# A state space layer reordered: norm, bias and rotation in PSUM banks, fewer steps per angle, another loop order

## The reference, cut to what matters

```
Bm, Cm = rmsnorm(x @ WB.T) * Bn_w + B_bias, rmsnorm(x @ WC.T) * Cn_w + C_bias     # per head, 128 columns
dt, lam = softplus(x @ Wdt.T), sigmoid(x @ Wlam.T)
angle = cumsum over t of (x @ Wth.T) * dt
Bm, Cm = rope(Bm, angle), rope(Cm, angle)
alpha = exp(-dt * exp(A_log)); beta = (1 - lam) * dt * alpha; gamma = lam * dt
h[t] = alpha[t] h[t-1] + beta[t] B[t-1] x[t-1]' + gamma[t] B[t] x[t]'
y[t] = C[t] . h[t]
out = (y * silu(z)) @ Wout.T,   z = x @ Wz.T;   x = x + out
```

## Time and profile before

| | us |
|---|---|
| median of 3 runs (1844.03 to 1847.19) | 1845.42 |
| the profiled execution, its own time | 1846.38 |
| its span | 1844.7 |
| TensorE busy | 1529.5 (83%) |
| VectorE busy | 1137.8 (62%) |
| ScalarE busy | 863.2 (47%) |
| GpSimd busy | 498.3 (27%) |

### The profile page before, as it was taken

How to read it: one execution, slowest core, us unless ns; L and a number is a source line. 1 busy time by engine, 2 the same in 40 slices (tenths; PEclk the granted TensorE clock), 3 DMA queues, 4 the chain that set the end, 5 groups by cost and what they waited for, 6 DMA issues and landing times. The chain is left out here.

```text
span 1844.7 us, 25358 instructions
## 1 busy us (share of the span) xinstructions
PE 1529.5 (83%) x8808; PEld 1090.0 (59%) x8808; DVE 1137.8 (62%) x2334; ACT 863.2 (47%) x1937; POOL 498.3 (27%) x515
## 2 busy tenths in 40 slices
PE   7869888589968995746999999999976688888768
PEld 5643444367645784644877787777832255555567
DVE  5778998356745545553456644444439678888833
ACT  2548898311335421222434442333324578888711
POOL 2350000000000031014243233224000288888810
PEclk9978999789979997577999999999989889999969
DMA  3007999554032001030000000000022222223010
GB/s 126 1 1 138 180 187 177 154 169 155 27 67 59 24 1 35 15 118 1 1 1 1 1 1 1 1 1 1 1 91 89 89 70 83 90 78 94 1 48 27
DMA packets 190491, 110.89 MB, mean 60 GB/s; under 512 B 150121, under 2 KB 166505, under 8 KB 189468
## 3 DMA queue, kind: packets, MB, share of 16 engines
q1 hardware_dynamic: 190364, 109.26, 23.0%
HBM read 75.41 MB, written 0.26 MB: 41 GB/s over the span
## 5 line engine op out<-in xcount | busy, mean ns | idle before, releaser
L670 DVE TENSOR_REDUCE x_row_max<-banks 128x1 f32<-128x512 f32 x248 | 152.6, 682 | 16.3 <-PE banks L364 16.2
L210 PE MATMUL banks<-a_w_ring,x_normed_T 128*128 128x512 f32 x320 | 151.2, 613 | 13.2 <-DVEq L2916 5.6
L2870 POOL TENSOR_TENSOR a_t<-a_t,a_bias_ring 128x512 f32<-128x512 f32 x64 | 126.4, 1996 | 129.5 <-DVE a_t L2942 129.3
L573 ACT ACTIVATE x_v_full<-banks,x_neg_max,x_q_scale 128x1024 int16<-128x1024 f32 x128 | 153.4, 1202 | 16.6 <-DMA x_v_full<-x_v_full 7.5
L2215 PE MATMUL banks<-x_v,x_expsT 128*128 128x128 f32 x1088 | 148.6, 277 | 10.8 <-ACT x_expsT L2373 5.9
L2215 PEld LDWEIGHTS banks<-x_v,x_expsT 128*128 128x128 f32 x1088 | 134.0, 192 | 15.3 <-ACT x_expsT L2373 7.3
L2493 DVE TENSOR_REDUCE x_small<-banks 128x1 f32<-128x2048 f32 x32 | 73.3, 2292 | 86.2 <-PE banks L2196 86.2
L2300 POOL TENSOR_TENSOR x_t<-x_t 128x512 f32<-128x512 f32 (+1 forms) x48 | 54.4, 1134 | 259.9 <-DVE x_t L2475 259.9
L2196 PE MATMUL banks<-x_kT,x_qT 128*128 128x512 f32 x256 | 118.6, 607 | 4.7 <-ACT x_exps L2355 4.7
L364 PE MATMUL banks<-x_kT_parts,x_qT_int 64*128 64x512 bf16 x512 | 103.9, 409 | 5.4 <-DVE x_row_max L670 2.6
L210 PEld LDWEIGHTS banks<-a_w_ring,x_normed_T 128*128 128x128 f32 x320 | 59.9, 195 | 79.9 <-issue 67.8
(11 more groups left out here) (531 smaller groups left out, 3595.2 us busy)
## 6 DMA issues: line engine op xcount, KB each, us to landing
a_w_ring<-in_L_attn_WB_T SPq DMA_DIRECT2D x16, 512.0 KB
a_w_ring<-in_L_attn_WC_T SPq DMA_DIRECT2D x16, 512.0 KB
f_w_gate_up<-in_L_ffn_gate_up SPq DMA_DIRECT2D x18, 352.0 KB
ctx_tokens<-in_ctx SPq DMA_DIRECT2D x16, 256.0 KB, 5.6
a_w_ring<-in_L_attn_Wth_T SPq DMA_DIRECT2D x8, 512.0 KB
a_bias_ring<-in_L_attn_B_bias_perm SPq DMA_DIRECT2D x16, 256.0 KB
a_bias_ring<-in_L_attn_C_bias_perm SPq DMA_DIRECT2D x16, 256.0 KB
f_w_down<-in_L_ffn_down SPq DMA_DIRECT2D x18, 176.0 KB
```

What stands on the lines that cost most here:

```text
L210: last = nc.tensor.matmul(out, lhsT, rhs, start=(i == 0), stop=(i == len(pairs) - 1))
L573: nc.scalar.activation(eb[:, q % RING], k.ps[:, 2 + 2 * (q % 2):4 + 2 * (q % 2), :].rearrange("p a n -> p (a n)"), ACT.Exp, bias=nb[:, v % ...
L670: nc.vector.reduce_max(mx[:, u % 2, i:i + 1], k.bank(MBANK[m % 3]), AX.X).then_inc(s.max_taken, 1)
L2870: last = nc.gpsimd.tensor_tensor(a, a, bring[:, i % RB, j], ALU.add).then_inc(s.bias_used, 1)
```

## The change

`l3_attn` is rewritten.

- The layer norm is inside the same block; the semaphores of the stage before are cleared by SP between loads (the two pools are swapped). DMA order: dt weights, A_log, Wz, ring pieces 0 and 1, Wx, piece 2, norm weights, Wout, clears, the rest.
- z is projected before theta 0 and 1, x after; weighting x and gating z are done between blocks of angles.
- Angles are in turns (dt divided by two pi once), so that the reduction is one rounding and one difference.
- Norm and bias are computed in place in the banks, both by VectorE, and the rotation reads the banks; `t1` goes. The sine product is one 512-column operation instead of two of 256 for each of B and C; GpSimd takes the halves crosswise.
- The root is a power of -0.5 on GpSimd, with the variance made by a copy on ScalarE; reciprocal and square root go. GpSimd masks E with a select.
- The diagonal of G isn't multiplied by TensorE: ScalarE sums each row of the diagonal matrix (accumulated copy), VectorE multiplies x_diag by it and adds it as it takes y.
- The order of the loop changes on every engine; three quarters of the output's gate, transposes and projection come before the last units end.

Its core (removed lines mostly left out):

```diff
-    BC_BANKS = ((1, 2), (0, 5))
+    HN = N4 // 2
+    CH = DIN // P
+    LAST = NG4 // CH * (CH - 1) * B
+    BC_BANKS = ((5, 6), (0, 1))
+    TH_BANKS, CUM_BANKS = (0, 1), (2, 3)
+    X_BANKS, Z_BANKS = (5, 4), (7, 6)
+    TURN_BANK, DECAY_BANK, G_BANK, Y_BANK = 3, 4, 2, 7
+    old = k.swap_pools()
...
+                for sem in old:
+                    sp.sem_clear(sem)
+                for i in range(3, NTH + NG4):
+                    piece(i)
...
+                def total_angle(q):
+                    pe.wait_ge(s.thdt_ready, q + 1)
+                    if q >= 2:
+                        pe.wait_ge(s.cum_taken, q - 1)
+                    nc.tensor.matmul(k.bank(CUM_BANKS[q % 2]), k.keep[:], thdt[:, q % 2], start=True, stop=True).then_inc(s.cum_in_psum, 1)
...
+                for q in range(NTH * B):
+                    total_angle(q)
+                    if q == 1:
+                        pe.wait_ge(s.ww_ready, 1)
+                        x_of(1)
+                    if q + 2 < NTH * B:
+                        theta(q + 2)
...
+                    for j in range(2):
+                        if n >= 2:
+                            pe.wait_ge(s.roped, 2 * (n - 2) + j + 1)
+                        matmul_acc(nc, k.bank(BC_BANKS[n % 2][j]), [(k.xt[:, c, tokens[b]], ring[:, i % RB, j, c]) for c in range(DC)]).then_inc(s.bc_in_psum, 1)
+                    if b == B - 1:
+                        pe.wait_ge(s.bc_in_psum, 2 * (n + 1))
+                        pe.sem_inc(s.w_used, 1)
...
+                def read_out(m):
+                    g, b = divmod(m, B)
+                    pe.wait_ge(t.e_masked, m + 1)
+                    if m >= 1:
+                        pe.wait_ge(t.y_taken, m)
+                    for h in range(HG):
+                        hh = g * HG + h
+                        last = nc.tensor.matmul(k.bank(Y_BANK, P, P4, h * P4), ee[:, m % 4, h * P:(h + 1) * P], xw[:, b, hh * P4:(hh + 1) * P4], start=True, stop=True)
+                    last.then_inc(t.y_in_psum, 1)
...
+                project(0)
+                for n in range(NU):
+                    if n == 0:
+                        pe.wait_ge(s.cum_taken, NTH * B)
+                    if n + 1 < NU:
+                        project(n + 1)
...
+                    if n >= 1:
+                        turn_over(n - 1, 0)
+                    decay(n)
+                    if n >= 1:
+                        turn_over(n - 1, 1)
                     if n >= 2:
+                        read_out(n - 2)
+                    if n >= 1:
+                        products(n - 1)
+                pe.wait_ge(t.yz_ready, B)
+                pe.wait_ge(s.roped, 2 * NU)
+                turn_over(NU - 1, 0)
+                y_turn(0, (0, 1))
+                turn_over(NU - 1, 1)
+                y_turn(1, (2,))
+                read_out(NU - 2)
+                products(NU - 1)
+                pe.wait_ge(k.w_loaded[10], 3 * 16)
+                pe.wait_ge(t.yT_ready, 2)
+                y_project((0, 1))
+                read_out(NU - 1)
+                y_project((2,))
+                pe.wait_ge(t.yz_ready, 2 * B)
+                y_turn(TURN_BANK, (3,))
+                pe.wait_ge(t.yT_ready, 3)
+                y_project((3,)).then_inc(t.y_out, 1)
...
+                    nc.scalar.activation(cosine, cosine, ACT.Sin, bias=quarter[:, 0:1], scale=-2.0 * PI_IN).then_inc(s.trig_done, 1)
+                    nc.scalar.activation(sine, sine, ACT.Sin, scale=2.0 * PI_IN).then_inc(s.trig_done, 1)
...
+                    act.wait_ge(s.sq_done, n + 1)
+                    nc.scalar.activation(st[:, r, 1], st[:, r, 0], ACT.Copy, bias=RMS_EPS, scale=1.0 / N4).then_inc(s.var_ready, 1)
...
+                def diagonal(m):
+                    act.wait_ge(t.e_masked, m + 1)
+                    if m >= 1:
+                        act.wait_ge(t.gd_ready, m)
+                    if m >= 2:
+                        act.wait_ge(t.gx_ready, m - 1)
+                    for h in range(HG):
+                        last = nc.scalar.activation(junk[:, 2, h * P:(h + 1) * P], dg[:, m % 2, h * P:(h + 1) * P], ACT.Copy, accum_out=gt[:, m % 2, h:h + 1])
+                    last.then_inc(t.gd_ready, 1)
+                act.wait_ge(s.ww_ready, 1)
+                decays(0)
+                squares(0)
+                for n in range(NU):
+                    if n >= 3:
+                        diagonal(n - 3)
                     if n + 1 < NU:
+                        decays(n + 1)
                         squares(n + 1)
+                    if n >= 1:
+                        take_turned(n - 1, 0)
+                    exponentials(n)
+                    if n >= 1:
+                        take_turned(n - 1, 1)
+                diagonal(NU - 3)
...
+                def root(n):
+                    pool.wait_ge(s.var_ready, n + 1)
+                    nc.gpsimd.tensor_tensor(st[:, n % 2, 2], st[:, n % 2, 1], neg_half[:], ALU.pow).then_inc(s.rstd_ready, 1)
+
+                def add_rotated(m):
+                    for j in range(2):
+                        pool.wait_ge(s.roped, 2 * m + j + 1)
+                        for hf, op in ((0, ALU.subtract), (1, ALU.add)):
+                            a = r1[:, m % 2, j, :, hf]
+                            last = nc.gpsimd.tensor_tensor(a, a, r2[:, j, :, 1 - hf], op)
+                        last.then_inc(s.added, 1)
+
+                def mask(m):
+                    pool.wait_ge(s.exp_done, m + 1)
+                    e4 = ee[:, m % 4].rearrange("p (h t) -> p h t", t=P)
+                    nc.gpsimd.affine_select(out=e4, in_=e4, compare_op=ALU.is_gt, fill=0.0, base=0, pattern=[[0, HG], [1, P]],
+                                            channel_multiplier=-1).then_inc(s.past_ready, 1)
+                root(0)
+                for n in range(NU + 1):
+                    if n >= 1:
+                        add_rotated(n - 1)
+                        mask(n - 1)
                     if n + 1 < NU:
                         root(n + 1)
...
+                def fraction(q):
+                    i, b = divmod(q, B)
+                    dve.wait_ge(s.cum_in_psum, q + 1)
+                    link(nc.vector.tensor_scalar(turn, k.bank(CUM_BANKS[q % 2]), ROUND, ROUND, ALU.add, ALU.subtract))
+                    nc.vector.tensor_tensor(sn[:, b, i * 8:(i + 1) * 8].rearrange("p h n -> p (h n)"), k.bank(CUM_BANKS[q % 2]), turn, ALU.subtract).then_inc(s.cum_taken, 1)
+                    dve.wait_ge(s.cum_taken, q + 1)
...
+                def norms(n):
+                    i = NTH + n // B
+                    dve.wait_ge(s.rstd_ready, n + 1)
+                    dve.wait_ge(slot[i % RB], need[i])
+                    for j in range(2):
+                        for h in range(HG):
+                            b4 = k.bank(BC_BANKS[n % 2][j], P, N4, h * N4)
+                            last = nc.vector.scalar_tensor_tensor(out=b4, in0=b4, scalar=st[:, n % 2, 2, j * HG + h:j * HG + h + 1], in1=nw[:, j], op0=ALU.mult, op1=ALU.mult)
+                        last.then_inc(s.normed, 1)
+                    for j in range(2):
+                        b4 = k.bank(BC_BANKS[n % 2][j])
+                        dve.wait_ge(s.normed, 2 * n + j + 1)
+                        nc.vector.tensor_tensor(b4, b4, bring[:, i % RB, j], ALU.add).then_inc(s.biased, 1)
+
+                def rotate(n):
+                    g, b = divmod(n, B)
+                    if n >= 2:
+                        dve.wait_ge(t.bcT_in_psum, 2 * (n - 1))
+                    for j in range(2):
+                        bc = k.bank(BC_BANKS[n % 2][j]).rearrange("p (h c n) -> p h c n", h=HG, c=2)
+                        dve.wait_ge(s.biased, 2 * n + j + 1)
+                        if n == 0 and j == 0:
+                            dve.wait_ge(s.trig_done, 2 * NTH * B)
+                        nc.vector.tensor_tensor(r1[:, n % 2, j], bc, cs[:, b, g * HG:(g + 1) * HG].unsqueeze(2).to_broadcast([P, HG, 2, HN]), ALU.mult)
+                        if n >= 1:
+                            dve.wait_ge(s.added, 2 * (n - 1) + j + 1)
+                        nc.vector.tensor_tensor(r2[:, j], bc, sn[:, b, g * HG:(g + 1) * HG].unsqueeze(2).to_broadcast([P, HG, 2, HN]), ALU.mult).then_inc(s.roped, 1)
+
+                def weigh(m):
+                    dve.wait_ge(s.past_ready, m + 1)
+                    dve.wait_ge(t.g_in_psum, m + 1)
+                    if m >= 2:
+                        dve.wait_ge(t.gd_ready, m - 1)
+                    nc.vector.tensor_tensor(dg[:, m % 2].rearrange("p (h t) -> p h t", t=P), k.bank(G_BANK).rearrange("p (h t) -> p h t", t=P),
+                                            k.ident[:].unsqueeze(1).to_broadcast([P, HG, P]), ALU.mult)
+                    nc.vector.tensor_tensor(ee[:, m % 4], ee[:, m % 4], k.bank(G_BANK), ALU.mult).then_inc(t.e_masked, 1)
+
+                def diagonal_x(m):
+                    g, b = divmod(m, B)
```

(25 more changed lines are left out.)

444 lines of the change are left out of this document (170 added, 274 removed).

## The result

The changed kernel takes 1743.2 us, the median of 4 runs (1739.8 to 1743.6); the kernel before took 1846.3 beside it. The ratio is 0.9438, 95% interval 0.9421 to 0.9455. The profiled execution took 1742.9 us with a span of 1741.1, so 103.6 less than the span before. The forecast was 1748, its range 1726 to 1786.

What follows compares the result with a forecast made beforehand. It took a loop of hand-offs, 9.3 us a unit, with GpSimd's bias between two parts of VectorE's work, to bound the kernel. Start and angles -45.2, loop -34 and end -19 made -98: 1846.4 to 1748 us, range 1726 to 1786.

Steps and rivals of the forecast that it cites:

- The three stretches of the sum: State space stage: start and angles to the first norm -45.2, loop -34, end -19 us, together -98.
- Loop, -34 forecast: First norm to thirty-second: 4.6, 29 periods of 8.3 and 6.8 make 252 us, against 286.1 before.
- The path that the prediction wrote down: Loop: TensorE's and ScalarE's projection, squares, copies, transposes and products interleaved through one transpose bank, 8.1 us a unit.
- Its signs: Included some 62 table loads gone, TensorE over 85% busy at full clock, TensorE waiting on ScalarE's copies, not GpSimd.
- The mark-up of 0.2: Loop period taken as 8.3 us instead of the summed 8.1, as three close engines are not always in time.
- Start and angles, -45.2 forecast: Stage start through angles and first unit: first norm at 1413.6 us against 1458.78.
- The term of 2.6 us a block: Angles: TensorE's six 512-column passes at 0.43 us bound a block, down from 4.60 us.
- End, -19 forecast: After the thirty-second norm: 19 us left of 38.2, with much diagonal and output projection work gone from there.
- The bound I put above, 8.4 a unit: VectorE's unit in the loop if writes to PSUM let nothing overlap; 7.2 us was taken.
- VectorE at 9.3 a unit: Rival, loop: VectorE binds through no overlap plus a wait at the diagonal's product with x; 1777 us, 20%.
- The angles at 3.5 a block: Rival, angles: product, rounding and sums wait in turn, so TensorE's pace is missed; 14 us more, 1762, 12%.
- The clock rival: Loop: TensorE's clock halves at the gap before C's transposes and stays, 5.0 us more a period; 1893 us, 3%.

Runs made afterwards that it cites:

- the last run: Changed kernel with the projection in halves between the transposes and without TensorE's wait for its own last matmul: 1717.2 us, ratio 0.9305.

## Why the prediction was right

The three stretches of the sum, -98, came to -41.8 - 42.5 - 18.8 = -103.1. Outside of them, the stage started 1.65 us later and the layer behind it was 2.1 shorter, which nearly cancel. The two misses in the sum, 3.4 too much and 8.5 too little, also cancel in part: that the total is 5 us off is better than its terms.

**Loop, -34 forecast, -42.5 measured** (first norm to thirty-second: 243.6 us against 286.1). The path that the prediction wrote down is the one that binds. Its signs came: of 62 loads of the root's and the exponential's tables one is left, TensorE is 92% busy at the full clock, and TensorE waits for ScalarE's copies. I summed 8.1 and took 8.3 for lateness among three close engines; there is none, every unit from the third projection on takes 7.93. Busy times a unit, from 1440 to 1560 us: VectorE 108.02 / 120 x 7.93 = 7.1 (7.2 forecast), ScalarE 6.4 (6.4), TensorE 7.3 (7.6), GpSimd 5.0 (5.4). The mark-up of 0.2 was mis-sized, and the sum before it by about as much: projection, second squares and variance, with their hand-offs, were put at about 5.1 and took 4.92.

**Start and angles, -45.2 forecast, -41.8 measured** (first norm 70.1 us after the stage's start against 111.9). The term of 2.6 us a block was 2.84. What I left out is TensorE's wait for its own last matmul at every second block: without it the block took 2.57. The gain of 2.0 a block was thus 1.76, and putting the six steps back costs these 1.76 again.

**End, -19 forecast, -18.8 measured**: 1662.24 to the residual at 1681.6. The parts agree in their sum; they were not compared one by one. No run undoes the inlined norm, the new order of the loads, or the early gate and projection, so what each of them brought at the start and in the end is not shown.

**GpSimd.** The power of eight columns took 1.64 us, in the bounds of 1.02 to 2.04 but nearer to the upper; the select over 512 columns 0.63, half of the four 128-column ones that I took. With nothing waiting for GpSimd neither mattered.

**VectorE's write to PSUM.** The bound I put above, 8.4 a unit, didn't come: a norm step is 0.351 us against 0.343, the eight take 2.17, and a sum in the bank runs like any operation with a PSUM input, 0.60 start to start. The unit is 7.1. The page "VectorE: DVE Perf Modes" of the Trainium skill, by whose errata section I estimated 7.6, is not borne out here, and the measurement decides: the rotation's product of 512 columns takes 0.681 us from a bank (`L3019`) and took 0.683 from SBUF in the kernel before (view by line: ns min/median/max, first to last start, form):

```profile
L2956 DVE TENSOR_TENSOR a_r<-a_t,a_cs x64: 677/683/1642, 1464.2 to 1757.0; 128x512 f32<-128x512 f32 x64
```

The prediction said that a PSUM input costs the same 0.68 as none, and named, which has no such row of 512 columns; this one bears it out. Written to SBUF the norm step is 0.336, so the place of the result is worth 0.015 us.

**The rivals.** VectorE at 9.3 a unit was wrong: it has 0.8 us a unit to spare, and even with two SBUF inputs, where it is full, the unit takes 8.03 at most. The angles at 3.5 a block were wrong. The clock rival had a right mechanism at twice its price (5.0 us a unit, for the whole unit at half speed; the mean loss was 2.4), and the wait that I put it on, about 0.8 us, does not do it by itself: with that wait the clock stays at 1.00. It fell with 1.77 us and then 0.70 idle in a unit, and, in about half of the units, with 0.74 and then 16 passes of 8 columns. So two parts of the change that I costed by their busy time alone, the table loads and the diagonal's passes, were worth more than that in this order.

**What failed in my reading of the kernel before.** I named GpSimd's bias, between two parts of VectorE's work, as what closes the loop of 9.3 us. Put back into the new order it costs 0.13 us a unit. It was part of a cycle that the order made, and in the new order it isn't one. The parts don't add up either: put back one at a time, loads and root cost 4.6 us a unit, the diagonal 1.5 and the bias 0.1, 6.2 together, while the whole loop gained 1.4. That suggests that the old order hid the table loads better than the new one can. At least the clock's part is the new order's: the kernel before had both loads and the 16 passes in each unit and ran at 1.00 from 1520 to 1700 us. The rest was only argued: how much of the old order's 9.23 us was due to which part, in that order, was not tried and stays open.

## What to carry to other kernels

Write down the chain of hand-offs through the scarcest buffer and add it up: an operation on it cost 0.52 of its 0.57 us a unit, one beside it (a power, a multiplication) at most 0.05, and a split of the longest item between two waits gave 17 us for no work. Cost a part in the order in which it will run: the two table loads with the root cost 4.6 us a unit in this order, about half of it TensorE's clock, and the diagonal's passes 1.54 in one place and 0.19 in another. And don't let an engine wait for its own last instruction only to tell another engine (2.84 us a block in the angles with it, 2.57 without); let the other one wait on that instruction's semaphore.

## What was not expected of the hardware

- TensorE's clock fell to the 1.2 GHz level in about half of the units of a loop in which the engine was 94% busy, with 16 passes of 8 columns in a row; the other units, with the same passes and waits, kept the full clock. The same passes in two groups of 8, with the wait filled, left it at 1.00, and so did 8 passes behind a wait of 0.74 us in the changed kernel, and 16 in a row in the kernel before.
- A 512-column select on GpSimd takes 0.63 us against 0.29 for 128 columns, and 0.73 for a sum of 256 columns. The power takes 1.64 us for 8 columns, and 2.09 beside VectorE's operations with two SBUF inputs. Of those, the ones that were disturbed took 1.1 to 1.7 us instead of 0.68.
- With TensorE and VectorE both full (the last run), VectorE's operations on banks show 0.72 instead of 0.68 us each.
